# A transformer block on one core: two PSUM banks change roles, and the gated global row reaches the residual by an accumulating transfer

## The reference, cut to what matters

```python
h = _layernorm(x) * (1 + ca) + sa
# attention, per segment of 128 tokens
local = softmax(Q @ K.T * SCALE) @ V
global_out = softmax(Qg @ Kg.T * SCALE) @ Vg       # one row for each segment
out = (local + global_out[:, :, None, :]) @ Wo.T + bo
x = x + ga * out
h = _layernorm(x) * (1 + cb) + sb
x = x + gb * experts(h)                            # top-1 of 16 experts, 512 tokens each at most
```

## Time and profile before

| | us |
|---|---|
| median of the runs | 1890.59 |
| profiled execution | 1888.11 |
| its span, first to last instruction | 1886.4 |
| PE busy | 1797.0 (95%) |
| DVE busy | 1224.1 (65%) |
| POOL busy | 868.4 (46%) |
| ACT busy | 821.9 (44%) |

### The profile page before, as it was taken

One profiled execution on the slowest core, in us unless ns is written; L12 is line 12 of the kernel. 1 busy time (PEld: TensorE's weight loads), 2 busy tenths in 40 slices (PEclk: granted clock), 3 DMA queues, 4 the chain that ended last, 5 costly groups with the idle time before them and its releaser, 6 DMA issues.

```text
span 1886.4 us, 28121 instructions
## 1 busy us (share of the span) xinstructions
PE 1797.0 (95%) x9137; PEld 1487.0 (79%) x9138; DVE 1224.1 (65%) x1882; ACT 821.9 (44%) x1322; POOL 868.4 (46%) x709
## 2 busy tenths in 40 slices
PE   8999999999999549999999999998998999999998
PEld 3677787787787437889888888887888988888886
DVE  4568888888887754555554554537757886455762
ACT  2544554554544323434434343336445564334541
POOL 2145655655655441334343432416637756233632
PEclk9999999999999779999999999999999999999999
DMA  8422432332342424343535434345545455434622
GB/s 279 140 90 90 150 119 90 133 135 89 115 164 82 176 68 164 126 142 128 187 141 174 145 123 145 117 164 183 175 141 206 165 212 180 156 122 156 223 81 67
DMA packets 137915, 270.77 MB, mean 144 GB/s; under 512 B 17633, under 2 KB 18221, under 8 KB 137862
## 3 DMA queue, kind: packets, MB, share of 16 engines
q1 hardware_dynamic: 115338, 221.27, 33.5%
q0 software_dynamic: 22528, 48.86, 8.0%
HBM read 237.71 MB, written 50.72 MB: 153 GB/s over the span
## 4 chain that ended last, share of the span: by engine, by line
PE 77%; DVE 11%; issue 4%; ACT 3%; POOL 2%; DMA 2%; SPq 1%; DVEq 0%; POOLq 0%; ACTq 0%
PE bank L323 23%; PE bank L325 23%; PE bank L324 23%; PE bank L762 2%; PE bank L698 2%; DVE prob L1260 2%; DVE h L1366 1%; DVE stats L1145 1%; DVE xr L1370 1%; PE bank L805 1%; PE bank L593 1%; DVE u_lo L1388 1%; PE bank L582 1%; DVE ht_lo L1206 1%; DMA g_x<-in_L_attn_x_dram 1%
## 5 line engine op out<-in xcount | busy, mean ns | idle before, releaser
L1427 DVE TENSOR_TENSOR h_lo<-h_f,h_hi 128x512 fp32r<-128x512 f32 x256 | 221.3, 885 | 363.5 <-ACT h_f L1079 363.4
L1078 ACT ACTIVATE h_hi<-bank,b_col 128x512 fp32r<-128x512 f32 x256 | 176.4, 689 | 598.1 <-PE bank L325 582.7
L323 PE MATMUL bank<-bt_hi,w_hi 128*128 128x512 f32 (+4 forms) x1024 | 360.7, 352 | 9.4 <-DVE w_lo L1398 5.5
L324 PE MATMUL bank<-bt_lo,w_hi 128*128 128x512 f32 (+4 forms) x1024 | 359.3, 351 | 0.0
L325 PE MATMUL bank<-bt_hi,w_lo 128*128 128x512 f32 (+4 forms) x1024 | 359.2, 351 | 0.0
L323 PE MATMUL bank<-w_hi,h_hi 128*128 128x512 f32 x832 | 325.9, 392 | 2.8 <-issue 2.7
L324 PE MATMUL bank<-w_lo,h_hi 128*128 128x512 f32 x832 | 324.2, 390 | 0.0
L325 PE MATMUL bank<-w_hi,h_lo 128*128 128x512 f32 x832 | 324.0, 389 | 0.0
L323 PEld LDWEIGHTS bank<-bt_hi,w_hi 128*128 128x128 f32 x1024 | 194.5, 190 | 35.5 <-issue 9.3
L324 PEld LDWEIGHTS bank<-bt_lo,w_hi 128*128 128x128 f32 x1024 | 194.6, 190 | 21.0
L325 PEld LDWEIGHTS bank<-bt_hi,w_lo 128*128 128x128 f32 x1024 | 194.4, 190 | 20.3
(11 more groups left out here) (265 smaller groups left out, 3224.3 us busy)
## 6 DMA issues: line engine op xcount, KB each, us to landing
raw<-in_L_ffn_W_dram SPq DMA_DIRECT2D x128, 1024.0 KB, 5.5
xa<-in_L_attn_x_dram SPq DMA_DIRECT2D x16, 1024.0 KB, 5.3
xr<-in_L_attn_x_dram SPq DMA_DIRECT2D x16, 1024.0 KB, 8.0
out_dram<-xr SPq DMA_DIRECT2D x16, 1024.0 KB, 10.0
h_rows<-h SPq DMA_DIRECT2D x16, 1024.0 KB, 4.3
b_bc<-in_L_ffn_b_dram SPq DMA_DIRECT2D x16, 256.0 KB, 6.3
wm_a<-in_L_wmod_dram SPq DMA_DIRECT2D x2, 1024.0 KB, 11.1
wm_b<-in_L_wmod_dram SPq DMA_DIRECT2D x2, 1024.0 KB, 11.3
```

The lines of the kernel that those rows point to most:

```text
L323: pe.matmul(o, a_hi, b_hi, start=start, stop=False)
L324: pe.matmul(o, a_hi, b_lo, start=False, stop=False)
L1078: act.activation(h1_hi[b % 2][:, j, :], h_bank[j][:, :], ACT.Relu, bias=bias)
L1427: dve.tensor_tensor(h1_lo[b % 2][:, j, :], h1_f[:, j, :], h1_hi[b % 2][:, j, :].bitcast(F32), ALU.subtract) \
```

## The change

It has two parts.

**The banks.** The last quarter of the transposed x no longer goes to `big[3]` but to a bank of its own, `t1_last` (the former bank of the scores); only in group 0 it stays in `big[3]`. The scores go to `big[3]`. So the last quarter doesn't wait for `u_split`; the scores do, and whatever goes into `big[3]` next (the second h2 transpose, or g tile 3) waits for the exponentials. PE's transposes of the logit parts move from before the scores to behind the first g tile of the next iteration. ACT modulates the next group before it copies the logit parts.

**The global row.** In the prologue a product of a selector (`seg_batch`) and the modulation rows gives the gate `ga` for each of the 64 segments; one DVE product gives `ga * global row` in fp32 (`g_ga`), which is stored to DRAM (128 KB). The bf16 matmul of line 726, its operands and the loads of `grows` go away. Instead POOL issues one transfer per group that adds the four rows, each broadcast to 128 partitions, into `xr` (1 MB written). DVE waits for this transfer instead of for the load of `xr`. POOL issues it at the start of its iteration, for group 0 behind the normalisation of group 2.

```diff
-    big, (s_bank, pt_bank, lg_bank, pos_bank) = banks[:4], banks[4:]
+    big, (t1_last, pt_bank, lg_bank, pos_bank) = banks[:4], banks[4:]
+    s_bank = big[3]
...
+    def t1_bank(g, k):
+        return t1_last if k == KC - 1 and not (isinstance(g.n, int) and g.n == 0) else big[k]
...
-        sp.dma_start(global_dram.rearrange("(n t) d -> n t d", t=3), g_split[:]).then_inc(g_stored, 16)
+        sp.wait_ge(g_gated, 1)
+        sp.dma_start(global_dram, g_ga[:]).then_inc(g_stored, 16)
...
-                wait_past(sp, av_full, 4 * i.n - 4)
-                sp.dma_start(grows[i.par][0:3 * GS, :], global_dram[bass.ds(i.n * 3 * GS, 3 * GS), :]) \
-                    .then_inc(grows_in[i.par], 16)
...
             for k in range(KC):
-                if not first:
+                if not first and k < KC - 1:
                     pe.wait_ge(u_split, 4 * g.n - 4 + k + 1)
                 for s in range(GS):
-                    last = pe.transpose(big[k][:, chunk(s)], xa[g.par][:, s, chunk(k)], ident[:])
+                    last = pe.transpose(t1_bank(g, k)[:, chunk(s)], xa[g.par][:, s, chunk(k)], ident[:])
...
+        pe.wait_ge(mod_fixed, 2)
+        pe.wait_ge(made, POOL_MADE)
+        bank_free(GAROW)
+        product(GAROW, pe.matmul(pro_bank(GAROW)[0:NSEG, :], seg_batch[:], modr[:, GA, :], start=True, stop=True))
...
                 g_tile(i, 0)
+            if prev3:
+                pe.wait_ge(parts_out, i.plus(-3).n + 1)
+                if prev2:
+                    pe.wait_ge(pt_split, p2.n + 1)
+                stand_alone(pe, pe_passed)
+                wait_past(pe, lg_step, i.plus(-3).n)
+                for s in range(GS):
+                    last = pe.transpose(pt_bank[:, chunk(s)], logit_parts[:, chunk(s)], ident[:])
+                last.then_inc(lg_full, 1)
+            if g_tiles:
                 g_tile(i, 1)
...
+                    if prev and big[(k + 2) % 4] is s_bank:
+                        pe.wait_ge(exp_done, 4 * p1.n + 4)
                     for s in range(GS):
                         last = pe.transpose(big[(k + 2) % 4][:, chunk(s)], h2[p2.par][:, s, chunk(k)], ident[:])
...
+                elif prev:
+                    pe.wait_ge(exp_done, 4 * p1.n + 4)
                 g_tile(i, 3)
...
-                pe.wait_ge(grows_in[p1.par], 16 * (p1.half + 1))
...
-                    split3(pe, big[s][:, :], pt_hi[:, s, :], pt_lo[:, s, :], u_hi[:, s, :], u_lo[:, s, :], True, False)
-                    pe.matmul(big[s][:, :], seg_sel[:, s, :], grows[p1.par][:], start=False, stop=True) \
+                    split3(pe, big[s][:, :], pt_hi[:, s, :], pt_lo[:, s, :], u_hi[:, s, :], u_lo[:, s, :], True, True) \
                         .then_inc(av_full, 1)
...
                 transpose_xn(i.plus(1), False)
-            if prev2:
-                pe.wait_ge(parts_out, p2.n + 1)
...
             if cur:
                 pe.wait_ge(gt_done, 4 * n + 4)
+                pe.wait_ge(u_split, 4 * n + 4)
...
+            if nxt:
+                modulate(i.plus(1))
             if prev2 and cur:
                 empty_parts()
-            if nxt:
-                modulate(i.plus(1))
...
-        dve.tensor_copy(g_split[:, 0, :], g_a[:]).then_inc(gsum_step, 1)
-        dve.wait_ge(gsum_step, 8)
-        dve.tensor_tensor(g_x[:], g_a[:], g_split[:, 0, :], ALU.subtract).then_inc(gsum_step, 1)
-        dve.wait_ge(gsum_step, 9)
-        dve.tensor_copy(g_split[:, 1, :], g_x[:]).then_inc(gsum_step, 1)
-        dve.wait_ge(gsum_step, 10)
-        dve.tensor_tensor(g_split[:, 2, :], g_x[:], g_split[:, 1, :], ALU.subtract).then_inc(g_split_done, 1)
+        dve.tensor_tensor(g_ga[:], g_a[:], g_b[:], ALU.mult).then_inc(g_gated, 1)
...
-                dve.wait_ge(xr_in[p1.par], 16 * (p1.half + 1))
+                dve.wait_ge(xr_summed[p1.par], 16 * (p1.half + 1))
...
         def iteration(i, prev, nxt, prev3):
             p1 = i.plus(-1)
             b = batch_of(p1)
+            def add_global():
+
+                pool.wait_ge(xr_in[p1.par], 16 * (p1.half + 1))
+                stand_alone(pool, pool_passed)
+                part = global_dram[bass.ds(p1.n * GS, GS), :].unsqueeze(0).to_broadcast([P, GS, D])
+                pool.dma_start(xr[p1.par][:], part, accum_op=ALU.add).then_inc(xr_summed[p1.par], 16)
+
+            first = isinstance(i.n, int) and i.n == 1
+            if prev and not first:
+                add_global()
             if nxt:
                 normalise1(i.plus(1))
+            if first:
+                pool.wait_ge(g_stored, 16)
+                add_global()
```

More of the change, by code:

```diff
@@ L82, in build_block @@
     qc_dram = nc.dram_tensor("query_consts", (NBATCH, 1), F32, kind="Internal").ap()
-    global_dram = nc.dram_tensor("global_rows", (NSEG * 3, D), BF16, kind="Internal").ap()
+    global_dram = nc.dram_tensor("global_rows", (NSEG, D), F32, kind="Internal").ap()
     h2_dram = nc.dram_tensor("h2_rows", (T, D), F32, kind="Internal").ap()
@@ L123, in build_block @@
     ones = keep("ones", [P, P], BF16)
-    seg_sel = keep("seg_sel", [P, GS, P], BF16)
-    grows = [keep(f"grows{i}", [P, D], BF16) for i in range(2)]
+    seg_batch = keep("seg_batch", [NBATCH, NSEG], F32)
     QUAD = P // KC
@@ L199, in build_block @@
                                       ("bqk", [NBATCH, 2, D], F32), ("hg_t", [P, KC, NSEG], F32))
-    g_split, brow, u_row, gg_t = over(r_tab + 8 * KB, ("g_split", [NSEG, 3, D], BF16), ("brow", [P, D], F32),
+    g_ga, brow, u_row, gg_t = over(r_tab + 8 * KB, ("g_ga", [NSEG, D], F32), ("brow", [P, D], F32),
                                       ("u_row", [1, D], F32), ("gg_t", [P, KC, NSEG], F32))
@@ L262, in build_block @@
     gsum_masked, gsum_negb, gsum_exp, gsum_prob = (sem(f"gsum_{k}") for k in ("masked", "negb", "exp", "prob"))
-    g_split_done, g_stored, table_cleared = sem("g_split_done"), sem("g_stored"), sem("table_cleared")
+    g_gated, g_stored, table_cleared = (sem(k) for k in ("g_gated", "g_stored", "table_cleared"))
     x_in = [sem(f"x_in{i}") for i in range(2)]
     xr_in = [sem(f"xr_in{i}") for i in range(2)]
-    grows_in = [sem(f"grows_in{i}") for i in range(2)]
+    xr_summed = [sem(f"xr_summed{i}") for i in range(2)]
     ln1_step, ln1_ready, ln1_rstd, xn_done = (sem(k) for k in ("ln1_step", "ln1_ready", "ln1_rstd", "xn_done"))
@@ L325, in split3 @@
         return pe.matmul(o, a_lo, b_hi, start=False, stop=stop)
-    (MCH, SCT, BCOL, FIRST4, WOT, UCOL, MCOL, VCH, HGT, LATE4, GROWS, GGT, SG, BROW, PGT, TG, B1T,
-     PRO_END) = (0, 4, 5, 6, 7, 11, 12, 13, 17, 18, 19, 20, 21, 22, 23, 24, 25, 26)
+    (MCH, SCT, BCOL, FIRST4, WOT, UCOL, MCOL, VCH, HGT, LATE4, GROWS, GGT, SG, BROW, PGT, GAROW, TG, B1T,
+     PRO_END) = (0, 4, 5, 6, 7, 11, 12, 13, 17, 18, 19, 20, 21, 22, 23, 24, 25, 26, 27)
     def pro_bank(q):
@@ L341, in build_block @@
     POOL_MADE = 9
-    DVE_MADE = 9
+    DVE_MADE = 7
     def results_done(eng, e, b):
@@ L417, in _ @@
         sp.dma_start(mod_dram[:, 0:VC, :], modr[:, 0:VC, :]).then_inc(mod_stored, 16)
-        sp.wait_ge(g_split_done, 1)
-        sp.dma_start(global_dram.rearrange("(n t) d -> n t d", t=3), g_split[:]).then_inc(g_stored, 16)
+        sp.wait_ge(g_gated, 1)
+        sp.dma_start(global_dram, g_ga[:]).then_inc(g_stored, 16)
         sp.wait_ge(mod_stored, 16)
@@ L744, in iteration @@
                 last.then_inc(parts_full, 1)
+            if cur and not g_tiles:
+                pe.wait_ge(pro_evac, PRO_END)
             if nxt:
                 transpose_xn(i.plus(1), False)
-            if prev2:
-                pe.wait_ge(parts_out, p2.n + 1)
[L749 to L755, removed]
             if cur:
-                if not g_tiles:
-                    pe.wait_ge(pro_evac, PRO_END)
                 pe.wait_ge(gt_done, 4 * n + 4)
+                pe.wait_ge(u_split, 4 * n + 4)
                 for s in range(GS):
@@ L776, in _ @@
         iteration(Group(NG // 2, 1), False, False, True, False, True)
-        ranks(Group(NG // 2 - 1, 1))
+        iteration(Group(NG // 2 + 1, 0), False, False, False, False, True)
         def rows_of(e):
@@ L945, in modulate @@
                 for rows in (ht_hi, ht[g.par]):
-                    ins = act.activation(rows[:, k, :], big[k][:, :], ACT.Identity,
+                    ins = act.activation(rows[:, k, :], t1_bank(g, k)[:, :], ACT.Identity,
                                          bias=mod_col[:, 0, k, bass.ds(batch_of(g), 1)],
@@ L986, in _ @@
         copy_out(PGT, pg_t[:], pro_bank(PGT)[0:NSEG, 0:NSEG])
+        copy_out(GAROW, g_b[:], pro_bank(GAROW)[0:NSEG, :])
         copy_out(TG, g_a[:], pro_bank(TG)[0:NSEG, :])
@@ L1122, in _ @@
         dve.memset(count[:], 0.0).then_inc(init_made, 1)
-        dve.memset(grows[0][:], 0.0).then_inc(init_made, 1)
-        dve.memset(grows[1][:], 0.0).then_inc(init_made, 1)
         dve.memset(pg[:], 0.0).then_inc(init_made, 1)
@@ L1265, in query_const @@
                 .then_inc(qc_ready, 1)
-        dve.wait_ge(g_split_done, 1)
```

(11 more changed lines are left out.)

## The result

The change costs 7 us. The kernel after takes 1898.39 us (median of 6 runs, 1897.04 to 1899.83) against 1891.28 us for the kernel before in the same session; the ratio is 1.0039, with a 95% interval of 1.0028 to 1.0049. One execution of before took 6576 us and one beside the experiments 8230 us; the ratios leave both out, and without the first the median of before is 1890.59 us and the cost 7.8 us. The forecast was 1896.4 us. The profiled execution of after took 1899.83 us (span 1898.2), that of before 1888.11 (span 1886.4). That difference of 11.8 us is larger than the measured one, and the first step is to find out which part of it is not the change.

The account below looks back on a forecast made before the run. Each steady group was taken as two halves, one bound by TensorE, one by VectorE. -5 (groups) - 1.4 (prologue) + 8.4 (group 0) + 3.8 (group 15) = +5.8 us: 1893.9 profiled, 1896.4 median; range 1888 to 1930.

Parts of the forecast that it names:

- prologue: Before the groups, one VectorE product replaces four instructions, so LayerNorm of group 1 starts earlier: 1.4 us gained, bounds 1.0 to 1.6.
- group 0's add: At group 0, the add issued behind POOL's normalisation of group 2 stalls VectorE's residual 8.4 us, bounds 4.7 and 12.1.
- group 15's add: At group 15, the add meets the h store and weight loads: 3.8 us late, bounds 0 and 10.
- groups, line 726 and exchange: Over the groups, removing the global-row matmul and exchanging banks together gain 5 us, bounds 1 to 6.
- steady adds: In steady groups the add lands just in time for VectorE's residual and costs nothing.
- The add: POOL's 1 MB accumulating transfer takes 8 us, bounds 4.3 and 11.7, plus 2.2 beside the h store.
- Line 726: In VectorE's half, the removed matmul's 0.92 us a group mostly becomes waiting; at most 0.08 a group, about 1 us, is gained.
- The exchange: At the third and fourth quarter, dropping the last quarter's wait gains 0.375 us in some 12 groups: 4.5 us.
- TensorE's half: In each steady group, from the third quarter to the transposes of prob, the chain runs on TensorE without a gap.

Follow-up runs that it names:

- banks: Kernel before with only the exchange of the banks; line 726's matmul stays, no accumulating transfer. Ratio 0.9984 to the kernel before, 3.0 us faster.
- no_add: Kernel after without the accumulating transfer, so the global term is missing from the output. Ratio 0.9934 to the kernel before, 12.5 us faster.
- row_only: Kernel after with scores and last quarter in their banks of before. Ratio 1.0039 to the kernel before, 7.4 us slower.
- adds_ahead: early_and_hold with group 0's xr loaded ahead of group 2's x, last add issued ahead of POOL's h2 work for group 14. 1884.3 us, ratio 0.9965.
- early_and_hold: Kernel after, group 0's add issued ahead of POOL's normalisation of group 2, weight loads held until group 15's add lands. Ratio 0.9993 to the kernel before.
- ahead_row: adds_ahead without the exchange of the banks. Ratio 0.9976 to the kernel before, 2.1 us above adds_ahead.
- cut_before: Kernel before without VectorE's four products of the query constant in each group. Ratio 1.0016 to the kernel before.

## Why the prediction was right, and where it was not

The direction and the size held, by the mechanism that had decided them: the add is late where nothing covers it, at the first and the last group. Term by term, from the stage:

| term | forecast | measured |
|---|---|---|
| prologue | -1.4 | -1.5 |
| group 0's add | +8.4 | +8.0 |
| group 15's add | +3.8 | +3.65 |
| groups, line 726 and exchange | -5 | -3.4 |
| group 1's add | none | +1.7 |
| steady adds | 0 | +0.9 |
| groups 14 to 15, without the add | none | -1.7 |
| sum | +5.8 | +7.7 |

That the sum is off by only 1.9 us is in part luck. Group 1's add (+1.7) and the clock between groups 14 and 15 (-1.7) were both missing from the forecast and cancel. And the -3.4 us of the groups stand near the -5 for another reason than mine: the exchange alone gave 0.3 us from group 0 to 14 (banks), not 4.5, so by difference some 3 us are left for line 726 and its loads, to which I had given 1. No run takes these out without anything else.

(-3.4 is no_add less before from group 0 to 14, -1.7 the same from group 14 to 15: before has its transposes, prob transposes and first products at 0.50 there, after and no_add only 32 score matmuls at a lower clock.)

- **The add.** 8 us alone, from a range of 4.3 to 11.7, was right: it took 7.8 us in after and 8.5 in row_only. So was 8 + 2.2 beside the h store: 10.1 in most groups, and up to 11.4. The Trainium skill, Collectives: The Full Stack, section "The bandwidth ceiling: the fold count and why AG ≠ RS ≠ AR", puts the halved rate of a ReduceScatter down to the two source reads of its add; carried over to this transfer, that is an estimate of 6.5 us. The measured 7.8 is 1.3 above it, so the halved rate alone isn't the whole price here. A third transport of 2.2 us would give 8.7, and nothing here tells what the 1.3 are. The issue shows 1 us on POOL, as for a scatter of 128 descriptors.
- **Group 15** had the right size by a partly wrong reason. I let the weight loads take half of the engines. Held back, they give 0.9 us at most; the rest is the add beside a store and its late place in POOL's queue: issued ahead of the h2 work in adds_ahead it isn't late at all. The working had a slip too: 8 us with 4.4 more of transport are 12.4 and not 12.1. The add took 11.0.
- **Line 726.** Right that it turns into a wait. The seven waits of the earlier trace rows told the bound of that half, and 0.92 us put back cost 0.09. Taken out, with no add in its place (no_add, which has the exchange too), it gave somewhat more than my 0.08 us a group: 428.50 us against 430.50 from group 2 to 14, 0.17 a group.
- **The exchange** is the step that failed. I took 1.25 us for eight transposes against 0.875 for eight out of a run of sixteen. But the third quarter keeps its wait, and without the wait between them the two quarters still take 1.09, so starting after a wait costs these eight about 0.2 us. Of the 0.16 us that are left, 0.1 arrives at the h2 transposes (in the chain of waits 10.74 us from the third quarter on before, 406.46 to 417.20, and 10.65 after, 415.83 to 426.48). It doesn't shorten the group: in banks it comes back as TensorE's longer wait before the third quarter. Over twelve groups nothing can be measured.
- **Group 1** was missing. I had looked at the first add and at the steady ones. But what makes group 0 late also makes POOL's h2 work of group 0 late, and group 1's add is queued behind that: issued at 139.16, 10.9 us to land, so 150.1, where no_add's distance from group 0 (113.76 + 34.48) gives 148.2.
- **"TensorE's half"** was too simple. It isn't one engine's: 0.92 us put into it cost 0.43, and the 0.1 us that the exchange took out of it gave nothing.

## What to carry to other kernels

A transfer that takes the place of work on an engine is priced at its first and last use, where the pipeline has no slack: the steady groups paid 0.9 us for twelve adds here, four others 13.3. Put its issue in front of what it needn't wait for, in the queue of the engine that issues it. And when a wait names an engine as the bound, taking work off that engine may only move the wait to the next thing the same engine makes: try the two savings together before dropping either.

## What the runs showed of the hardware

- An adding transfer of 1 MB from four broadcast rows of DRAM into SBUF took 7.8 us (after), 8.2 (early_and_hold) and 8.5 (row_only) at group 0, with no store beside it. In the other groups of after, beside the 1 MB store of h, it took 10.1 to 11.4, and 11.0 where four weight loads ran too. The store of h next to it takes 5.2 us in the median instead of 4.3.
- TensorE's granted clock falls to its lower level for single stretches after it has stood still (1.8 us in ahead_row, 3.65 in before), and which instructions meet it moves the stage by 1.6 to 2.2 us: 32 score matmuls took 3.7 to 3.8 us or 5.1 to 5.4. How long it stood still doesn't decide it alone, as the last scores of after and then of adds_ahead show. With one profile of each kernel, such a gain or loss can't be put down to an edit.

```profile
631.14 5.44 PE L772 MATMUL bank<-ht,gt 128*128 128x128 f32 x32 [2.70 <-DVE u_lo L1390]
...
622.43 3.81 PE L775 MATMUL bank<-ht,gt 128*128 128x128 f32 x32 [2.69 <-DVE u_lo L1393]
```

- A VectorE operation of 128 x 4 elements took 0.17 us just behind POOL's normalisation and 0.70 beside it, ending with it. An ht_lo, 128 x 512, took 0.69 us with POOL idle; beside POOL's h2 products the two of before took 3.14 together and the 32 of cut_before from 300 to 588 us 1.76 each in the median.
